# First rounds of the pair stage: v products of the first pair behind the second round's scores, modulation steps moved, one output part sooner

## What is computed

```
mod = (silu(c) @ wmod).reshape(4, 6, 1, 256)        # sa, ca, ga, sb, cb, gb
h = layernorm(x) * (1 + ca) + sa
x = x + ga * attention(h)                            # block 0: 16 heads of 64, causal softmax, k and v from a latent of rank 128
h = layernorm(x) * (1 + cb) + sb
x = x + gb * low_rank_feed_forward(h)
# block 1: the same frame (its own c and wmod) round a linear causal attention with an MLP and a routed feed-forward
```

## Time and profile before

| | us |
|---|---|
| median of 3 runs | 1707.37 (1707.13 to 1708.22) |
| profiled execution, its own time | 1711.82 |
| its span | 1710.4 |
| TensorE busy | 1662.8 (97%) |
| VectorE busy | 1224.5 (72%) |
| ScalarE busy | 846.6 (49%) |
| GpSimd busy | 868.3 (51%) |

### The profile page before, as it was taken

One profiled execution on the slowest core, in us unless ns is written; L12 is line 12 of the kernel. 1 busy time (PEld: TensorE's weight loads), 2 busy tenths in 40 slices (PEclk: granted clock), 3 DMA queues, 4 the chain that ended last, 5 costly groups with the idle time before them and its releaser, 6 DMA issues.

```text
span 1710.4 us, 41069 instructions
## 1 busy us (share of the span) xinstructions
PE 1662.8 (97%) x16550; PEld 1138.0 (67%) x16550; DVE 1224.5 (72%) x2674; ACT 846.6 (49%) x1872; POOL 868.3 (51%) x1127
## 2 busy tenths in 40 slices
PE   9999999999999999999999999999999999999997
PEld 5566685768566667566856667756784666766666
DVE  4898957636699994762779997675468999676444
ACT  5667624223576763422457775432246767443232
POOL 3788852232188884232228888314114888740420
PEclk9999999999999999999999999999999999999999
DMA  6566572231666655041356665405045666620504
GB/s 188 124 157 154 139 187 84 39 61 41 161 152 142 148 142 167 1 72 28 87 136 156 150 144 134 146 2 99 1 122 134 145 149 146 157 101 2 99 0 125
DMA packets 143853, 189.11 MB, mean 111 GB/s; under 512 B 34512, under 2 KB 107696, under 8 KB 142640
## 3 DMA queue, kind: packets, MB, share of 16 engines
q1 hardware_dynamic: 125472, 179.14, 42.7%
q10 hardware_dynamic: 18192, 7.35, 1.8%
HBM read 88.32 MB, written 13.16 MB: 59 GB/s over the span
## 4 chain that ended last, share of the span: by engine, by line
PE 76%; DVE 12%; ACT 4%; POOL 3%; issue 2%; DMA 1%; SPq 1%; ACTq 0%; POOLq 0%; DVEq 0%
PE scores L470 13%; PE scores L666 12%; PE bank L688 11%; PE bank L470 5%; PE bank L710 5%; PE bank L714 3%; PE bank L720 3%; ACT prob L917 2%; DVE prob L801 2%; POOL placed L865 2%; PE scores L441 2%; PE scores L1782 2%; PE scores L1722 2%; DVE hx L801 1%; DVE stats L297 1%
## 5 line engine op out<-in xcount | busy, mean ns | idle before, releaser
L865 POOL COPY placed<-prob 32x768 f32<-32x768 f32 x448 | 367.8, 821 | 208.2 <-DVE prob L801 166.2
L301 POOL TENSOR_TENSOR rstd<-rstd,minus_half 128x2 f32<-128x2 f32 (+1 forms) x100 | 71.5, 715 | 491.7 <-DVE rstd L300 489.5
L688 PEld LDWEIGHTS bank<-placed,v_t 128*64 128x64 f32 x4608 | 255.0, 137 | 38.9 <-issue 38.7
L666 PE MATMUL scores<-k_t,q_t 64*128 64x512 f32 (+3 forms) x1536 | 274.7, 497 | 2.9 <-DVE neg_max L794 2.9
L688 PE MATMUL bank<-placed,v_t 128*64 128x128 f32 x4608 | 269.3, 273 | 1.6 <-DMA placed<-prob 1.5
L801 DVE STREAM_TRANSPOSE prob<-prob 128x1536 f32<-128x1536 f32 x128 | 220.0, 1757 | 37.2 <-ACT prob L917 37.2
L794 DVE CUSTOM_DVE_ANT_0 mod_rows<-scores,hx 128x128 f32<-128x128 f32 (+7 forms) x256 | 190.7, 745 | 37.7 <-PE scores L666 37.1
L666 PEld LDWEIGHTS scores<-k_t,q_t 64*128 64x128 f32 x1536 | 130.8, 187 | 117.0 <-issue 95.7
L865 POOL COPY placed<-hx 32x768 f32<-32x768 f32 x224 | 184.0, 822 | 30.2 <-DVE hx L801 13.3
L917 ACT ACTIVATE prob<-mod_rows,neg_max 128x128 f32<-128x128 f32 (+2 forms) x192 | 137.3, 715 | 120.0 <-DVE neg_max L794 117.0
L794 DVE CUSTOM_DVE_ANT_0 x<-scores,hx 128x128 f32<-128x128 f32 (+7 forms) x256 | 192.6, 752 | 0.0
(11 more groups left out here) (252 smaller groups left out, 3114.5 us busy)
## 6 DMA issues: line engine op xcount, KB each, us to landing
placed<-prob SPq DMA_DIRECT2D x576, 96.0 KB, 2.5
f<-in_L_ffn_f SPq DMA_DIRECT2D x16, 2048.0 KB, 13.5
placed<-hx SPq DMA_DIRECT2D x288, 96.0 KB, 2.2
inverse_wide<-inverse_scratch SPq DMA_DIRECT2D x64, 256.0 KB, 4.3
slots_scratch<-high_rows SPq DMA_DIRECT2D x16, 512.0 KB, 6.5
inter<-slots_scratch SPq DMA_DIRECT2D x32, 256.0 KB, 4.8
mod_rows<-mod_scratch SPq DMA_DIRECT2D x32, 128.0 KB, 5.0
out<-x SPq DMA_DIRECT2D x16, 256.0 KB, 2.1
```

Source lines behind the costliest of these rows:

```text
L301: step = pool.do(lambda e, ts=ts: nc.gpsimd.tensor_tensor(rstd[:, ts], rstd[:, ts], minus_half[:, ts], op=ALU.pow), var, filled)
L666: last = nc.tensor.matmul(score_tiles[head][:, at_ // 512, at_ % 512:at_ % 512 + hi - lo], q_t[buf][rows_, tile * P:(tile + 1) * P], k_t[b ...
L688: last = nc.tensor.matmul(out_bank[rows_, at_:at_ + P], v_t[pair % 2][:, j, rows_], placed[m % 2][:, :, head, first_block(m, i) + j, :], s ...
L865: nc.gpsimd.tensor_copy(placed[m % 2][target * GROUP:(target + 1) * GROUP, source, :, :, :], prob[m % 3][source * GROUP:(source + 1) * GRO ...
```

## The change

- The v jobs of the first pair leave the stretch before round 0 and are made in round 1, behind scores(1). Round 1 then has the jobs v0, v1 of the first pair and k0, k1 of the second; round 2 has v0 and v1 of the second pair, both in `job_bank`.
- The banks of the first pair's and of the early jobs are dealt anew: halves 1 use `out_bank`, halves 0 `job_bank`.
- `mod_products` is behind scores(0), `mod_read` in round 0, `mod_columns` still behind scores(2) but in `out_bank` (waiting for the read of k1), `mod_values` at the end of round 3, `mod_turn` in round 4. values(0) waits for `mod_take`.
- ScalarE reads the first pair's v0 and v1 at the head of round 1, ahead of its exponentials, and in round 3 it reads q0 right after the exponentials of the first tile.
- `output_part(0)` moves from round 22 to round 21.
- The loads of weights wait for the last product that reads the part they overwrite, not for all jobs of that pair.

```diff
         def jobs_of(m):
             pair = m // ROUNDS_OF + 1
-            return [(pair, j) for j in JOBS if round_of(pair, j) == m] if pair < PAIRS else []
+            return [(p, j) for p in (0, pair) for j in JOBS if round_of(p, j) == m] if pair < PAIRS else []
         def round_of(pair, j):
-            return ROUNDS_OF * (pair - 1) + (JOBS.index(j) // 2 if (pair, j) != (1, "v0") else 1)
+            return ROUNDS_OF * (pair - 1) + JOBS.index(j) // 2 if pair else 1 if j[0] == "v" else -1
         def in_out_bank(pair, j):
-            if pair and round_of(pair, j) >= FILLING:
-                return False
-            return int(j[1]) == (0 if pair else 1)
+            return int(j[1]) == 1 and (pair == 0 or round_of(pair, j) < FILLING)
         def job_number(pair, j):
-            return len(JOBS) * pair + JOBS.index(j) + 1
-
-        def jobs_ahead(m):
-            return [] if b == 0 and m == 2 else jobs_of(m)[:1]
+            later = 2 if (pair, j[0]) == (0, "v") else -2 if (pair, j[0]) == (1, "q") else 0
+            return len(JOBS) * pair + JOBS.index(j) + 1 + later
...
-        MOD_ROUND = 3
+        MOD_ROUND = 4
...
# pe_pairs, values
+                if b == 0 and m == 0:
+                    e.wait_ge(flow["mod_step"], 1)
# pe_pairs, job
-                if pair == 0 and kind == "v":
-                    e.wait_ge(flow["job_read_act"], base["job_read_act"] + job_number(0, JOBS[2 + half]))
-                elif pair:
+                if m >= 0:
                     e.wait_ge(flow["job_read_act"], base["job_read_act"] + bank_read_ahead_of(pair, j))
-                    if b == 0 and m == 1:
-                        e.wait_ge(flow["mod_read"], 1 if out else 2)
-                    if b == 0 and m == 2:
-                        e.wait_ge(flow["mod_step"], 1)
+                    if b == 0 and m == 0:
+                        e.wait_ge(flow["mod_read"], 2 if out else 1)
...
             def mod_columns():
-                e.wait_ge(flow["job_read_act"], bank_read(2, False))
+                e.wait_ge(flow["job_read_act"], bank_read(2, True))
...
             for m in range(ROUNDS):
                 scores(m)
-                if b == 0 and m == 1:
+                if b == 0 and m == 0:
                     mod_products()
                 if b == 0 and m == 2:
                     mod_columns()
-                ahead = jobs_of(m) if m < FILLING else jobs_ahead(m)
+                ahead = jobs_of(m) if m < FILLING else jobs_of(m)[:1]
                 for j in ahead:
                     job(*j)
+                if m == ROUNDS - 3:
+                    output_part(0)
                 if m == ROUNDS - 1:
                     output_part(1)
-                if m == ROUNDS - 2:
-                    output_part(0)
# dve_pairs
-                if b == 0 and m == 2:
+                if b == 0 and m == 3:
                     mod_values()
# act_pairs
-                    e.wait_ge(flow["job_done"], base["job_done"] + (pair - 1) * len(JOBS))
+                    read_last = ("q1", "k1", "v1")[m % ROUNDS_OF]
+                    e.wait_ge(flow["job_done"], base["job_done"] + job_number(pair - 2, read_last))
...
-            for j in JOBS:
+            for j in JOBS[:4]:
                 job(0, j)
...
-                ahead = jobs[:1] if m == 1 else jobs_ahead(m) if m >= FILLING else []
+                ahead = jobs[:1] if m >= FILLING else []
...
+                if m == 1:
+                    for j in jobs[:2]:
+                        job(*j)
+                    jobs = jobs[2:]
                 for i in range(large):
                     for head in range(HEADS):
                         exponential(m, i, head)
+                    if i == 0 and m == 3:
+                        job(*jobs.pop(0))
+                        ahead = []
...
-                if b == 0 and m == 1:
+                if b == 0 and m == 0:
                     mod_read()
-                early = m == 1 or len(tiles_in(m)) > 2
+                early = len(tiles_in(m)) > 2
```

More of the change, by code:

```diff
@@ L636, in bank_read @@
         def bank_read(m, out):
-            jobs = [(0, "v1" if out else "v0")] + [j for n in range(min(m, ROUNDS)) for j in jobs_of(n)]
+            jobs = [(0, "k1" if out else "k0")] + [j for n in range(min(m, ROUNDS)) for j in jobs_of(n)]
             return job_number(*[j for j in jobs if in_out_bank(*j) == out][-1])
         def bank_read_ahead_of(pair, j):
-            jobs = [(0, "v0"), (0, "v1")] + [k for n in range(ROUNDS) for k in jobs_of(n)]
+            jobs = [(0, "k0"), (0, "k1")] + [k for n in range(ROUNDS) for k in jobs_of(n)]
             jobs = [k for k in jobs if in_out_bank(*k) == in_out_bank(pair, j)]
             return job_number(*jobs[jobs.index((pair, j)) - 1])
-        MOD_ROUND = 3
+        MOD_ROUND = 4
         MOD_CHUNK, MOD_ROWS = 4 * P, (QR - 1) * VPAD + NB
@@ L733, in mod_products @@
             def mod_products():
-                e.wait_ge(flow["job_read_act"], job_number(*jobs_of(0)[1]))
+                e.wait_ge(flow["job_read_act"], job_number(0, "k1"))
                 e.wait_ge(loaded["wmod0"], 16)
@@ L737, in mod_products @@
                     for r, (l, at_) in enumerate(MOD_CHUNKS[:QR]):
-                        nc.tensor.matmul(job_bank[r * VPAD:r * VPAD + NB, :], silu[:, l, cc, :],
+                        nc.tensor.matmul(out_bank[r * VPAD:r * VPAD + NB, :], silu[:, l, cc, :],
                                          wmod[l][:, cc, at_:at_ + MOD_CHUNK], start=cc == 0, stop=cc == C - 1)
@@ L742, in mod_products @@
                     for r in range(QR):
-                        last = nc.tensor.matmul(out_bank[r * VPAD:r * VPAD + NB, 0:P], silu[:, l, cc, :],
+                        last = nc.tensor.matmul(job_bank[r * VPAD:r * VPAD + NB, 0:P], silu[:, l, cc, :],
                                                 wmod[l][:, cc, at_ + r * P:at_ + (r + 1) * P], start=cc == 0, stop=cc == C - 1)
@@ L747, in mod_columns @@
             def mod_columns():
-                e.wait_ge(flow["job_read_act"], bank_read(2, False))
+                e.wait_ge(flow["job_read_act"], bank_read(2, True))
                 for q in range(QR + 1):
-                    last = nc.tensor.transpose(job_bank[:, q * MOD_ROWS:(q + 1) * MOD_ROWS], mod_raw[q], ident[0:MOD_ROWS, 0:MOD_ROWS])
+                    last = nc.tensor.transpose(out_bank[:, q * MOD_ROWS:(q + 1) * MOD_ROWS], mod_raw[q], ident[0:MOD_ROWS, 0:MOD_ROWS])
                 last.then_inc(flow["mod_columns_made"], 1)
@@ L761, in pe_pairs @@
                     return job(0, JOBS[m])
-                if kind == "keys and values":
-                    return [job(0, j) for j in JOBS[2:]]
+                if kind == "first keys":
+                    return [job(0, j) for j in JOBS[2:4]]
                 return values(m)
@@ L817, in mod_take @@
                     at_ = q * MOD_ROWS
-                    groups = job_bank[:, at_ // VPAD * VPAD:at_ // VPAD * VPAD + P].rearrange("p (r w) -> p r w", w=VPAD)
+                    groups = out_bank[:, at_ // VPAD * VPAD:at_ // VPAD * VPAD + P].rearrange("p (r w) -> p r w", w=VPAD)
                     last = nc.vector.tensor_copy(late[:, 0:QR, q, :] if q < QR else late[:, QR, :, :],
@@ L940, in mod_read @@
                 e.wait_ge(flow["mod_made"], 1)
-                nc.scalar.copy(mod_raw[QR], out_bank[0:MOD_ROWS, 0:P]).then_inc(flow["mod_read"], 1)
-                nc.scalar.copy(mod_rows[0:MOD_ROWS, 0:2, :].rearrange("p k n -> p (k n)"), job_bank[0:MOD_ROWS, :]
+                nc.scalar.copy(mod_raw[QR], job_bank[0:MOD_ROWS, 0:P]).then_inc(flow["mod_read"], 1)
+                nc.scalar.copy(mod_rows[0:MOD_ROWS, 0:2, :].rearrange("p k n -> p (k n)"), out_bank[0:MOD_ROWS, :]
                                ).then_inc(flow["mod_read"], 1)
@@ L1037, in batch @@
         sp.do(sp_pairs)
-        pe.do(lambda e: pe_pairs(e, ("keys and values", 0)), *banks.readers[0:2], *lat_done)
+        pe.do(lambda e: pe_pairs(e, ("first keys", 0)), *banks.readers[0:2], *lat_done)
         pe.do(pe_pairs, *banks.readers, *silu_late)
```

## The result

The changed kernel takes 1719.3 us (median of 4 runs, 1717.5 to 1722.1) against 1707.8 (4 runs, 1707.1 to 1709.1). The ratio is 1.0064, 95% interval 1.0051 to 1.0076. The direction was the forecast's; the size was not: +6.3 us was predicted, to 1717.5 at most.

A forecast was written before the change was run, and what follows sets the result against it. TensorE was taken as the bound, losing time only when it waits or runs at lower clock; +3.3, +1.9, +1.9, +1.4 for the batches, -0.8 output part, -1.4 clock made +6.3 on 1707.4: 1713.7 us, range 1707.5 to 1717.5.

The forecast's parts named there:

- Part 1: First pair's v products behind scores(1), batches 1 to 3: v1 of round 2 waits, scores(3) come 1.9 us later.
- Part 2: q0's early read in round 3, all batches: ScalarE waits 1.4 us, k1 of round 4 waits 0.5 to 0.7.
- Part 3: Batch 0 with the modulation steps moved: idle of about 3 us before k1 of round 4, 1.2 GHz behind it, +3.3.
- Part 4: Output part 0 one round sooner: the 0.35 us wait ahead of scores(22) goes, 0.2 per batch, -0.8 us in all.
- The clock term: Ends of block 1's attention: one 1.2 GHz stretch fewer than the three of four batches before, -1.4 us.
- the two that the prediction named as a sign of being wrong: Ends of batches: the forecast is wrong if 1.2 GHz stretches there fall by more than two.
- The starting point: Median of the kernel before, 1707.4 us, to which the forecast difference was added.
- Rival C: Batch 0: a second 1.2 GHz stretch, and no fewer at the batch ends, +9.7 us, 1717.1 us; chance 0.07.
- Rival B: Fill bound by VectorE's first scores: everything starts 1.03 us sooner per batch, -6.4 us, 1701.0 us; chance 0.15.

The follow-up runs named there:

- run 8: The kernel before with v0 of the second pair in round 2, in the job bank with v1: +1.2 ± 0.8 us at equal clock.
- run 5: The changed kernel with ScalarE's read of q0 in round 3 back ahead of the last tile: 5.9 us (± 1.3) faster than the changed kernel.
- run 9: The changed kernel with q0's read in round 3 behind the second tile's exponentials instead of the first's: 5.5 us (± 1.3) faster than the changed kernel.
- run 2: The kernel before with q0 in round 3 read right behind the first tile's exponentials: 0.4 ± 0.7 us faster than the kernel before.
- single undoings: The changed kernel with one edit taken back each: q0's early read 5.9 us faster, first pair's v products 4.2, modulation arithmetic 1.5, output part 0.7.
- Run 1: The kernel before with output part 0 in round 21 instead of 22: no measurable difference, -0.1 ± 0.7 us.
- run 3: The changed kernel with output part 0 back in round 22: 0.7 us (± 1.5) faster than the changed kernel.
- run 6: The changed kernel with the modulation arithmetic back at the end of round 2, batch 0: 1.5 us (± 1.5) faster than the changed kernel.

## Why the prediction was right in direction and wrong in size

**Part 1, the wait of v1 (right as a wait, wrong as a price).** 2.0 us of idle was forecast ahead of v1 in batch 1, 2.12 measured; scores(0) 0.86, measured 0.78; scores(3) 23 us behind scores(0), measured 22.96. "Scores(3) 1.9 us later", read as a cost that TensorE keeps, was the wrong step: run 8 has that wait, and most of the lag is back by scores(6). The loss in batches 1 to 3 came out near the forecast (3.6 with a 1.2 GHz stretch in it, 1.9, 2.0; forecast 1.9, 1.9, 1.4), but partly by luck: v1's wait was priced too high, and the early read of q0, counted as nothing more, made up for it.

**Part 2, q0's early read (mechanism right, weight wrong).** ScalarE's wait was foreseen at 1.4 (measured 1.45), k1's wait at 0.5 to 0.7 (0.71). The prediction called TensorE unfeeling of it and let it add nothing to v1's 1.9. **This is the step of the mechanism that failed**: it is the largest single piece, and without it 5.9 of the 10.1 us go (run 5; 5.5 in run 9). In the kernel before it is free to within the bounds (run 2), because scores(3) are there 3.6 us ahead of the minima of round 3; in the changed one only 2.0. Run 8 shows that v0's move alone does this (batch 1, scores(3) at 473.25, 477.42 and 474.76):

```profile
476.85 0.25 DVE L794 CUSTOM_DVE_ANT_0 mod_rows<-scores,hx 128x128 f32<-128x128 f32 x1
...
479.47 0.25 DVE L788 CUSTOM_DVE_ANT_0 mod_rows<-scores,hx 128x128 f32<-128x128 f32 x1
...
476.80 0.25 DVE L794 CUSTOM_DVE_ANT_0 mod_rows<-scores,hx 128x128 f32<-128x128 f32 x1
```

The lines are of the kernel before, the changed one and run 8. That these two edits together cost what neither costs alone (-0.4 in run 2, +1.2 in run 8) follows from the traces; no run times the two alone. The shares of the single undoings (5.9, 4.2, 1.5, 0.7) add up to more than the whole.

**Part 3, batch 0 (mechanism right, the clock's price too low).** Idle of 1.0, 1.5, none and 3.0 us were forecast; 0.77, 1.14, none and 3.35 measured. The arithmetic took 1.86 us behind the transposes of round 3 (63.50 to 65.36), as the 1.8 forecast; but both of the two instructions that the prediction compares (0.69 and 0.17) read one operand of 128x32 elements, so that only the first was held up by GpSimd is an inference which no run tests. That 1.2 GHz would follow the long stall was right, its length not: 5.6 us of it, some 2.8 us lost instead of 1.3. Scores(5) at 71.95, measured 71.89, is in part luck: this execution had no 1.2 GHz in the prologue, so scores(0) came at 24.60 and not 25.43. From scores(0) on batch 0 lost 4.4, net of that 3.5, against 3.3.

**Part 4, the output part (a gain that is given back).** -0.8 was forecast. The gain ahead of scores(22) came (0.4 per batch), but waits of 0.77, 0.37, 0.65 and 0.69 came ahead of the rest of the output: its norms wait for the last pair's inverse row sums, which ScalarE stores. The working stopped at the next values and never followed to the end of the stage. Run 1 puts the term at -0.1 ± 0.7, run 3 at +0.7 ± 1.5: 0.7 to 1.5 us of the miss.

**The clock term (the term of the sum that failed most plainly).** "Three of four is more than a shifted start should meet; I count one less: -1.4" took a stretch away from the median of the runs, though it had been counted in the profiled execution, which was 4.4 us above that median and had more of them. The profile of the changed kernel did have three fewer (none for three), by more than the two that the prediction named as a sign of being wrong; the runs do not bear it out. Their mean clocks, 0.9959 over 77 and 0.9955 over 4, make it +0.4 us, with ±1.3 for the four: no gain that shows.

**The starting point.** Three runs gave 1707.4; 77 give 1709.0. The forecast inherits 1.6 us.

In sum, of the 5.6 us of the miss 1.6 are the start, 1.4 the clock term and 0.7 to 1.5 the output part; the 1.1 to 1.9 left are not attributed, and the four runs of the changed kernel carry ±1.1 by themselves. The upper end of the range had no room for a low starting median. Rival C (+9.7) came nearest in number, but not as described: batch 0 had one longer stretch at 1.2 GHz, not two. Rival B falls: scores(0) did come 1.03 us sooner, and nothing was won by it. Its argument counts 4.8 us from scores(2) to the minima by the prediction's sum; the prediction's own times (464.9 and 469.9) give 5.0, and nothing hangs on it.

## What to carry to other kernels

Where a wait moves when an edit removes it, the bound is elsewhere: follow the engines that feed the waiting one, and price an edit by what it adds to their chain, not by the idle time that it makes or removes. An early read of a product is free only while the product is there first; in front of the binding engine's work its wait lengthens the chain (here 1.45 us in a stage or more, and 5.9 us in all), so check every "sooner" against the latest time its operand can arrive after all the other edits. Before adding a difference to a median, ask whether the profiled execution was a typical one.

## What the runs showed of the hardware

The same kernel scatters from 1705.7 to 1711.6 us over 77 runs on three occasions, and the mean granted clock goes with it (0.96 us per 0.001). Waits of 2.40 (run 2), 2.84 (before) and 3.35 us (changed) were followed by 3.4, 3.4 and 5.6 us at 1.2 GHz, waits of 1.28 and 1.43 us ahead of k1 in round 4 (runs 6, 5) by none. But a stretch also came without a long wait: at the end of block 1's attention the same cluster of waits, 0.27, 0.49, 0.40 and 0.47 us, was followed by 1.2 GHz in batch 0 of the profile before (first line) and by full clock in that of the changed kernel (second line):

```profile
336.18 0.96 PE L441 MATMUL scores<-ident,hx 128*128 128x128 f32 x5 [0.47 <-DVE hx L308]
...
340.15 0.76 PE L441 MATMUL scores<-ident,hx 128*128 128x128 f32 x5 [0.47 <-DVE hx L308]
```

At this size a comparison of two profiles says little about 3 us (6.9 between the profiles, 10 between the runs).
